# A scan's state moved from PSUM to SBUF, and the first and last tiles reordered, in a fused attention and FFN kernel on one Trainium2 core

## The reference

```python
k = rope(x @ Wk.T);  v = x @ Wv.T            # per head: (16 tokens, 32) blocks
W0 = eye(32)
def step(W, kv):                             # 256 steps, one after the other
    kc, vc = kv
    z = kc @ W
    grad = kc.T @ ((z - vc) * (2.0 / (16 * 32)))
    return W - grad, z
out = layernorm(zs) * gamma + beta
x = layernorm(x + out @ Wo.T)
hdn = silu((x @ gate_w.T) * gate_s) * ((x @ up_w.T) * up_s)
x = layernorm(x + (hdn @ down_w.T) * down_s)
```

## Time and profile before

| | us |
|---|---|
| median of 3 runs | 2057.38 |
| lowest and highest of them | 2052.96, 2057.82 |
| the profiled execution | 2071.61 |
| its span (first to last instruction) | 2069.7 |
| first `scan_z` of tick 1 (start of the scan) | 89.75 |
| first `scan_z` of tick 2, tick 3 | 133.31, 212.71 |
| first `scan_z` of tick 32, end of its last slot | 1923.55, 1975.14 |

### The profile page before, as it was taken

The page is one execution under the profiler, slowest core; times in us unless marked ns, Lnnn a source line. Parts: engine busy times, 40 slices in busy tenths (PEclk is TensorE's granted clock), DMA queues, the critical chain, the costliest instruction groups (busy, mean ns, idle before and its releaser), DMA issues.

```text
span 2069.7 us, 53846 instructions
## 1 busy us (share of the span) xinstructions
PE 1869.2 (90%) x21656; PEld 1460.7 (71%) x21656; DVE 1300.4 (63%) x2878; ACT 914.4 (44%) x2258; POOL 641.1 (31%) x778
## 2 busy tenths in 40 slices
PE   3235999999999999999999999999999999999887
PEld 2123777777777777777777777777777777777765
DVE  2247676667666766676666667666676676666642
ACT  1122544444444444444444444444444444444422
POOL 1001233332333333323323333233333333333222
PEclk8677999999999999999999999999999999999999
DMA  5574444454555444544544445445444454444320
GB/s 188 191 221 142 135 143 143 140 153 128 148 157 153 139 137 140 153 132 145 157 150 130 147 141 150 134 145 155 144 140 146 142 149 130 149 146 147 93 78 27
DMA packets 314194, 294.02 MB, mean 142 GB/s; under 512 B 42968, under 2 KB 264408, under 8 KB 313944
## 3 DMA queue, kind: packets, MB, share of 16 engines
q1 hardware_dynamic: 302048, 272.21, 44.2%
q10 hardware_dynamic: 11896, 18.35, 2.7%
HBM read 156.19 MB, written 142.87 MB: 144 GB/s over the span
## 4 chain that ended last, share of the span: by engine, by line
PE 47%; DVE 24%; DMA 11%; issue 7%; SPq 4%; ACT 3%; POOL 2%; ACTq 1%; DVEq 0%; POOLq 0%
PE work L725 18%; PE gu_acc L739 16%; DVE err L925 9%; PE down_acc L751 8%; DMA landed<-zT_scr 5%; DMA zT_scr<-turned 4%; DVE hid L932 3%; DVE turned L864 3%; PE z_acc L698 2%; DVE stats L845 2%; DVE x_tok L859 2%; PE state_acc L713 2%; POOL rstd L431 2%; SPq L307 2%; SPq L261 2%
## 5 line engine op out<-in xcount | busy, mean ns | idle before, releaser
L453 POOL TENSOR_TENSOR hid_lo<-hid,hid_hi 128x256 fp32r<-128x256 f32 x352 | 261.8, 744 | 905.1 <-ACT hid_hi L544 905.1
L925 DVE TENSOR_TENSOR err<-z_acc,v_rows 32x256 f32<-32x256 f32 x1024 | 429.1, 419 | 113.8 <-PE z_acc L698 87.8
L510 ACT ACTIVATE state<-state_acc 32x256 f32<-32x256 f32 x1028 | 384.5, 374 | 76.3 <-PE state_acc L713 57.0
L739 PE MATMUL gu_acc<-x_hi,gw 128*128 128x256 f32 x1408 | 386.3, 307 | 34.0 <-DVE hid L932 30.9
L534 ACT ACTIVATE hid<-gu_acc,gate_scale 128x256 f32<-128x256 f32 x352 | 166.7, 474 | 413.0 <-PE gu_acc L739 412.2
L739 PE MATMUL gu_acc<-x_lo,gw 128*128 128x256 f32 x1408 | 348.1, 280 | 0.0
L739 PE MATMUL gu_acc<-x_hi,uw 128*128 128x256 f32 x1408 | 347.5, 280 | 0.0
L739 PE MATMUL gu_acc<-x_lo,uw 128*128 128x256 f32 x1408 | 346.9, 279 | 0.0
L739 PEld LDWEIGHTS gu_acc<-x_hi,gw 128*128 128x128 f32 x1408 | 265.3, 188 | 98.9 <-DVE hid L932 74.9
L932 DVE SCALAR_TENSOR_TENSOR hid<-gu_acc,up_scale,hid 128x256 f32<-128x256 f32 x352 | 168.8, 479 | 262.2 <-ACT hid L534 258.4
L751 PE MATMUL down_acc<-dw,hid_hi 128*128 128x512 f32 x704 | 281.8, 400 | 1.0 <-POOL hid_lo L453 1.0
(11 more groups left out here) (74 smaller groups left out, 2083.9 us busy)
## 6 DMA issues: line engine op xcount, KB each, us to landing
x_fm<-xT SPq DMA_DIRECT2D x64, 256.0 KB, 3.5
k_scr<-k_tok SPq DMA_DIRECT2D x32, 512.0 KB, 3.9
k_rows<-k_scr SPq DMA_DIRECT2D x512, 32.0 KB, 2.1
v_rows<-v_scr SPq DMA_DIRECT2D x512, 32.0 KB, 2.1
z_scr<-v_rows SPq DMA_DIRECT2D x32, 512.0 KB, 3.2
z_tok<-z_scr SPq DMA_DIRECT2D x512, 32.0 KB, 1.8
x_tok<-x SPq DMA_DIRECT2D x32, 512.0 KB, 3.8
zT_scr<-turned SPq DMA_DIRECT2D x128, 128.0 KB, 3.1
```

Of the source, the lines that this page charges most:

```text
L453: pool.tensor_tensor(hid_lo[m % RING][:], hid[m % 2][:], hid_hi[m % RING][:].bitcast(F32), ALU.subtract).then_inc(hid_lo_ready, 1)
L510: act.activation(state[q, :, e].rearrange("p (r g) e -> p r g e", r=2), state_acc[q, :, 0:P].rearrange("p r (g e) -> p r g e", e=HEAD), AC ...
L739: mm = pe.matmul(gu_acc[:, k * TOK:(k + 1) * TOK], lhsT=w[:, c, m * P:(m + 1) * P].bitcast(dt), rhs=part[:, c].bitcast(dt), start=(c == 0 ...
L925: dve.tensor_tensor(err[q, g:g + 2, :, :].rearrange("p a (r h) e -> p a r (h e)", r=2), z_acc[q, :, 0:P].rearrange("p r (a c) -> p a r c", ...
```

## The change

**The scan's state.** `state` is held in SBUF, begun by a DMA of an identity. `scan_state` writes only the gradient of one step to PSUM, as 16 products of 32 x 32 stationary operands (before: 8 products with 64 rows). The new `step_state` on VectorE multiplies it by -STEP or 0 (`half_step`) and adds it to `state`, in two instructions of 128 partitions; `copy_state` on ScalarE is gone. z, the gradient and the last tile's transposes share four banks, `scan_acc`; therefore a wait for `save_z` stands in the middle of `scan_state` and no longer ahead of `scan_z`. `scan_err` is one instruction of 128 partitions.

**FFN weights.** Six copies and six loads, issued by SP among the tiles' transfers in ticks -1 to 2, in place of three copies and nine loads by ScalarE. A piece is `128x2x1408` or `128x6x512`, partitions outermost; the copies of gate and up were `2048x1x352`. All twelve pieces of `weigh` stand in tick 2.

**First tile.** Its key transposes and the second half of the key rows go on SP, its value rows on ScalarE (`load_first_v`). The projection of its batch 1 keys is in tick -1.

**SP's order.** The load of x for tile o stands behind the store of zn, and the store of k behind the load of zn.

**Last tiles.** For the last tile, TensorE transposes zn and x1 into `scan_acc` (`turn_last`), with no DRAM round trip. From unit 3 of the last but one tile, every other `gate_up` uses a bank of `scan_acc`. New tables spread the FFN units of ticks 33 and 34 over the slots otherwise than in the usual ticks.

The core of the diff, with the moved tick lines left out:

```diff
-WEIGHED = {(1, 9): (0,), (1, 11): (1,), (1, 13): (2,), (1, 15): (3,), (2, 1): (4, 5), (2, 3): (6, 7), (2, 5): (8,),
-           (2, 9): (9, 10), (2, 10): (11,)}
...
+WEIGHED = {(2, 5): (0,), (2, 6): (1,), (2, 9): (2, 3), (2, 10): (4, 5), (2, 11): (6, 7), (2, 12): (8, 9), (2, 13): (10, 11)}
...
-        state_acc = bank_pair("state_acc")
-        z_acc = bank_pair("z_acc")
+        scan_acc = ctx.enter_context(nc.psum_tensor("scan_acc", [P, NG // 2, 512], F32))
+        z_acc = scan_acc[:, 2:4, 0:P]
+        step_acc = scan_acc[:, :, P:P + 2 * HEAD]
...
+            def copy_ffn(i, half):
+                dst, src = ((gw_scr, gwT), (uw_scr, uwT), (dw_scr, dwT))[i]
+                r = slice(*((0, DM // 2), (DM // 2, DM), (0, 6 * P), (6 * P, INTER))[half if i < 2 else half + 2])
+                sp.dma_start(dst[r].rearrange("(c p) n -> p c n", p=P), src[r].rearrange("(c p) n -> p c n", p=P)
+                             ).then_inc(ffn_copied[i], 16)
+            def load_ffn(i, half):
+                dst, src = ((gw, gw_scr), (uw, uw_scr), (dw, dw_scr))[i]
+                c = slice(*((0, NC // 2), (NC // 2, NC), (0, 6), (6, NM))[half if i < 2 else half + 2])
+                sp.wait_ge(ffn_copied[i], 32)
+                sp.dma_start(dst[:].bitcast(F32)[:, c], src.rearrange("(c p) n -> p c n", p=P)[:, c]
+                             ).then_inc(ffn_in[i], 16)
...
+                if t == 2:
+                    load_ffn(0, 0)
+                    load_ffn(0, 1)
+                if within(t):
+                    store_v(t, 0)
+                if within(o) and o != LAST:
+                    store_znT(o)
                 if within(o):
                     load_x(o)
-                if within(t):
-                    store_v(t, 0)
-                if within(o):
-                    store_znT(o)
+                if within(o) and o != LAST:
+                    load_znT(o)
+                if t == 2:
+                    load_ffn(1, 0)
                 if within(t):
                     store_k(t)
-                if within(o):
-                    load_znT(o)
-                if within(t):
                     store_v(t, 1)
+                if t == 0:
+                    store_kT(t)
+                    load_kT(t)
+                    load_k_half0(t)
+                    load_k_half1(t)
+                if t == 1:
+                    copy_ffn(2, 0)
+                if t == 2:
+                    load_ffn(1, 1)
                 if within(sc):
...
+                if t == -1:
+                    copy_ffn(0, 0)
+                if t == 0:
+                    copy_ffn(0, 1)
+                    copy_ffn(1, 0)
+                    copy_ffn(1, 1)
+                if t == 1:
+                    copy_ffn(2, 1)
...
-            def copy_state():
-                for h in range(HQ):
-                    q = slice(h * HEAD, (h + 1) * HEAD)
-                    e = slice(h % 2 * HEAD, (h % 2 + 1) * HEAD)
-                    act.activation(state[q, :, e].rearrange("p (r g) e -> p r g e", r=2),
-                                   state_acc[q, :, 0:P].rearrange("p r (g e) -> p r g e", e=HEAD),
-                                   ACT.Copy, scale=-STEP).then_inc(state_ready, 1)
...
-            def keep_state(n, i):
-                act.wait_ge(state_added, 4 * NS * n + 4 * i + 4)
-                copy_state()
...
+            def load_first_v():
+                act.wait_ge(v_stored, 32)
+                for half in range(2):
+                    for g in range(NG):
+                        b, hg = g // NC, g % NC
+                        act.dma_start(v_rows[g * MB:(g + 1) * MB, half * NS // 2:(half + 1) * NS // 2, g % 2, :],
+                                      v_scr[b, half * P // 2:(half + 1) * P // 2, hg * P:(hg + 1) * P]
+                                      .rearrange("(i t) c -> t i c", t=MB)).then_inc(rows_in[half], 16)
...
-                for r in range(2):
-                    k = slice(r * P // 2, (r + 1) * P // 2)
+                pe.wait_ge(err_ready, NS * n + i + 1)
+                for j in range(NG // 2):
+                    k = slice(j * HEAD, (j + 1) * HEAD)
+                    if j == 2:
+                        pe.wait_ge(z_saved, NS * n + i + 1)
                     for h in range(HQ):
                         q = slice(h * HEAD, (h + 1) * HEAD)
-                        mm = pe.matmul(state_acc[q, r, 0:P], lhsT=k_rows[k, i, q], rhs=err[k, :, h, :],
-                                       start=False, stop=False, skip_group_check=True,
-                                       tile_position=(r * P // 2, h * HEAD))
-                        if r:
+                        mm = pe.matmul(step_acc[q, j, :], lhsT=k_rows[k, i, q], rhs=err[k, :, h, :], start=True,
+                                       stop=True, skip_group_check=True, tile_position=(j * HEAD, h * HEAD))
+                        if j == NG // 2 - 1:
...
+            def turn_last(src, b, ready, done):
+                pe.wait_ge(ready, 2 * LAST + b + 1)
+                for c in range(NC):
+                    mm = pe.transpose(scan_acc[:, b, c * P:(c + 1) * P], src[:, b, c * P:(c + 1) * P], eye[:])
+                mm.then_inc(done, 1)
+            def turn_last_zn():
+                pe.wait_ge(state_ready, 2 * NS * NT)
+                for b in range(BATCH):
+                    turn_last(z_tok, b, zn_ready, zn_turned)
+            def turn_last_x1():
+                pe.wait_ge(zn_low, 2 * NT)
+                for b in range(BATCH):
+                    turn_last(x1_tok[LAST % 2], b, x1_ready, x1_turned)
...
                 if i % (NS // 2) == 0:
                     dve.wait_ge(rows_in[i // (NS // 2)], 256 * (n + 1))
-                for j in range(NG // 2):
-                    q = slice(j * HEAD, (j + 1) * HEAD)
-                    g = j % 2 * 2
-                    dve.wait_ge(z_done, 4 * NS * n + 4 * i + j + 1)
-                    dve.tensor_tensor(err[q, g:g + 2, :, :].rearrange("p a (r h) e -> p a r (h e)", r=2),
-                                      z_acc[q, :, 0:P].rearrange("p r (a c) -> p a r c", a=2),
-                                      v_rows[q, i].rearrange("p a (r c) -> p a r c", r=2),
-                                      ALU.subtract).then_inc(err_ready, 1)
+                dve.wait_ge(z_done, 4 * NS * n + 4 * i + 4)
+                dve.tensor_tensor(err[:].rearrange("p a (r h) e -> p a r (h e)", r=2),
+                                  z_acc.rearrange("p r (a c) -> p a r c", a=2),
+                                  v_rows[:, i].rearrange("p a (r c) -> p a r c", r=2),
+                                  ALU.subtract).then_inc(err_ready, 1)
+            def step_state(n, i):
+                dve.wait_ge(state_added, 4 * NS * n + 4 * i + 4)
+                for e in range(2):
+                    part = state[:, :, e * HEAD:(e + 1) * HEAD].rearrange("p (j o) e -> p j o e", o=2)
+                    dve.scalar_tensor_tensor(part, step_acc.rearrange("p j (o e) -> p j o e", o=2),
+                                             half_step[:, e:e + 1], part, ALU.mult, ALU.add).then_inc(state_ready, 1)
```

297 lines of the change are left out of this document (144 added, 153 removed).

## The result

| | before | after |
|---|---|---|
| median of 5 runs, us | 2057.38 | 2069.04 |
| lowest and highest, us | 2052.96, 2058.63 | 2065.14, 2073.38 |
| ratio to before (95% interval) | | 1.0068 (1.0048 to 1.0089) |

The changed kernel is slower by 0.7%. The prediction said 2001 us.

The account below looks back on a forecast made before the run. TensorE was taken as the bound in the 29 usual ticks, waits at the edges. Start -47, usual ticks +9, end -18 sum to -56: 2071.61 becomes 2015.6, less 14.2 for the profiled run's excess, about 2001 us; range 1957 to 2041.

Parts of the forecast that it names:

- Start: Everything before tick 3: its start would come at 166 us instead of 212.7, a gain of 47 us.
- Tick 2: Third part of the start: all twelve weight looks on VectorE would lengthen it from 79.4 to 85 us.
- rival (c): At the start, one SP queue carries copies, loads and tile traffic; tick 3 begins at about 200, total 2036 us; chance 0.16.
- Usual tick: Each of the 29 ticks from tick 3 on: +1.44 - 0.79 - 0.35 = +0.3 us, together +9 us.
- Slot 13: In each usual tick, VectorE's state update ahead of `rotate` makes TensorE's projection of v wait 1.44 us more.
- The wait for `hid`: In slots 8 to 10 of the usual tick, TensorE's `gate_up` wait for `hid` would go: -0.79 us a tick.
- The scan's products: In `scan_state`, 16 smaller products in place of 8 would take the same 0.45 us a step: change 0.
- rival (d): `scan_state` in 32 x 32 pieces takes double, +0.38 to 0.45 us a step over 256 steps: 2098 us; chance 0.05.
- zn's: Usual tick: zn's store no longer has a load of x ahead, so TensorE's wait falls 0.35 of 0.72 us.
- End: Tick 32 and the time after the scan: -7, -5 and -6 us, together -18; bounds -28 and -8.
- the bank: After the scan, a second bank for `gate_up` removes 0.31 us of TensorE idle time 18 times: -5 us.
- Tick 32: First part of the end: most of its 7.6 us of waits in the `err` and state chain goes, -7 us.

Follow-up runs that it names:

- the second profile: The kernel before, unchanged, profiled once more: span 2057.2 us, usual ticks 58.64 us instead of 58.99.

## Why the prediction was wrong

The miss is 68 us. By the steps of the sum, in the spans of the two profiles on record:

**Start, forecast -47, came -29.** The gain of the first tick was right: the first `scan_z` at 44.4 (48 forecast), tick 1 36.6 us (33). Tick 2 was the step that failed: 85 forecast, 102.7 came. I charged it for the looks alone, 6.5 us, and took the tiles' transfers to be as late as before. What stood in the order of SP, loads of weights ahead of zn, k and x1, was read and not costed. TensorE waits 9.5 us more for zn and 9.8 more for k_sin, which stands behind x1 and two of the looks, and the choice of the form, two slots later, is another 5.8. That is 25 us more in waits, less 8 us by which the scan's own waits are shorter; the remaining 6 of the 23 us are TensorE's own work, 45.0 instead of 39.6 us at a granted clock of 0.65 instead of 0.72. That the loads cause the two waits is read from SP's order in the trace; moving only the gate weights changed tick 2 by no more than the profiles scatter, and only the kernel with the whole start of before brought it to 71.8. The outcome is close to rival (c), whose mechanism was that one, with 200 us as its price, and the start alone came out between the two. One reading of the prediction was wrong without harm to the sum: it says that by the rule on the slowest dimension the slow copy would run on all 16 engines. That dimension is 4 in the copy's source, and it ran on four.

**Usual tick, forecast +0.3, came +1.07 (+1.42 against the second profile).** Slot 13 was right: 1.44 forecast, and in one tick the start of the projection of v behind the last `down` moved from 0.23 to 1.72 us, 1.49; the wait in the table is 37.2 us, 42 forecast. The wait for `hid`: -0.79 forecast, 22.9 to 1.1 us came, -0.75. The scan's products: 0 forecast, 228 ns a record against 225 for those of z, and one `scan_state` takes 0.33 us of TensorE where it took 0.38; rival (d) is dead. (The Trainium skill, "TensorE: Matmul & The Clock Gate", section on 56 ns, says that matmuls never start closer than about 25 ns: 32 records in 0.33 us, about 10 ns each, disagree, so the measurement decides.) The term that failed is zn's: -0.35 forecast, with +0.3 as the bad end, and +0.50 came (20.8 to 35.2 us; +0.63 against the second profile). I saw that the load of x no longer stood ahead of the store, and didn't ask what it stood ahead of now: the load of zn. The bound was too tight for the same reason; it was made for the store of k, which is neutral. With the load of x put back and nothing else, the kernel takes 0.984 of the kernel before, 2031 us, which lies inside the stated range.

**End, forecast -18, came -8.6 (-6.1 against the second profile).** Two gate_up units stand 2.84 us apart, as forecast, and the bank gave 3.4 to 4.4 of its 5 us, which leaves 2 to 5 us for TensorE's transposes and the new tables, where 6 was forecast. Tick 32 gave nothing (51.59 to 51.60), where -7 was forecast. Its waits before and after:

```profile
PE z_acc L698 <- ACT state L510: 3.4, 2, 2.0
PE state_acc L713 <- DVE err L925: 2.7, 2, 1.9
PE gu_acc L739 <- DVE hid L932: 1.5, 2, 0.8
```

```profile
PE scan_acc L708 <- DVE state L964: 2.8, 2, 2.3
PE work L736 <- DVE fm L983: 2.0, 1, 2.0
PE gu_acc L755 <- DVE hid L969: 0.8, 1, 0.8
PE scan_acc L725 <- DVE err L954: 0.7, 1, 0.7
```

The scan's waits fell from 6.1 to 3.5 us, not to nothing, since the update queues on VectorE behind z's statistics; a wait of 2.0 us for zn is new; and TensorE's own work is 1.0 us more (44.0 to 45.1).

**From span to median.** -47 + 9 - 18 = -56 was forecast and -6.8 came: 49 us of the 68. The other 18 are the two profiled runs, 14.2 over the median before and 3.9 under it after. Taking the 14.2 off the result was right for a forecast of the median. But of the 10 us that it had more in the usual ticks 3.8 were waits for zn, in the row that I counted as a gain to be had, and most of the rest was time at half the clock, which I didn't look for.

**The rivals.** None had two transfers collide on the path of zn. The one on the slower side was the wrong mechanism, and 0.93 for faster was far too sure: the terms of the start and of zn rested on one untested assumption, that a transfer moved in a queue costs nothing to its new neighbours.
